# A two-layer block (causal attention, then a product-key mixture of 1024 experts): scale moved into the selecting matrix, the best sixteen of both tiles taken together, the maximum's steps spread over three bank pairs

## What is computed

```python
def reference(x, w_attn, w_proj, gamma, wq, keys, table_down, table_up):
    x = x + attention(layernorm(x), w_attn, w_proj)   # 16 heads of 8, one shared key and value head, causal
    x = x + ffn(layernorm(x), ...)
    return x

def ffn(x, gamma, wq, keys, table_down, table_up):
    xn = rmsnorm(x, gamma)
    q = (xn @ wq.T)                       # two halves, 8 heads, width 64
    sim = einsum('pbnhd,hkpd->pbnhk', q, keys)        # 2 x 32 similarities a head
    sx, ix = top_k(sim[0], 16);  sy, iy = top_k(sim[1], 16)
    all_scores = sx[..., :, None] + sy[..., None, :]  # 16 x 16 pairs
    scores, pk = top_k(all_scores, 16)
    indices = (ix * 32 + iy)[pk]
    h = einsum('bnd,bnhkd->bnhk', xn, table_down[indices])
    h = gelu(h) * softmax(scores)
    return einsum('bnhk,bnhkd->bnd', h, table_up[indices])
```

## Time and profile before

| | |
|---|---|
| median of 3 runs | 893.08 us |
| the profiled execution: its own time | 894.57 us |
| its span, first to last instruction | 892.8 us |
| mean granted TensorE clock | 0.935 of full |
| busy: TensorE | 716.4 us (80%) |
| busy: VectorE | 761.1 us (85%) |
| busy: ScalarE | 708.2 us (79%) |
| busy: GpSimd | 648.8 us (73%) |

### The profile page before, as it was taken

The page is one execution under the profiler, slowest core; times in us unless marked ns, Lnnn a source line. Parts: engine busy times, 40 slices in busy tenths (PEclk is TensorE's granted clock), DMA queues, the critical chain, the costliest instruction groups (busy, mean ns, idle before and its releaser), DMA issues.

```text
span 892.8 us, 20720 instructions
## 1 busy us (share of the span) xinstructions
PE 716.4 (80%) x5972; PEld 471.3 (53%) x6004; DVE 761.1 (85%) x2966; ACT 708.2 (79%) x961; POOL 648.8 (73%) x371
## 2 busy tenths in 40 slices
PE   3787787888979797888979797978889797967454
PEld 2653345564746465565646464655647463635333
DVE  4328699989999898999899898989899898969596
ACT  1364888989889898989989898989898888856371
POOL 2111586997979696988979696969979795969470
PEclk9797889999999999999999999999999998978676
DMA  6323021211203021212103020212112020100000
GB/s 169 52 39 71 1 54 26 58 25 26 56 10 72 0 64 18 57 25 44 38 10 72 0 67 15 57 25 57 25 27 55 10 68 1 31 1 19 0 1 12
DMA packets 34736, 32.52 MB, mean 36 GB/s; under 512 B 5521, under 2 KB 32785, under 8 KB 32977
## 3 DMA queue, kind: packets, MB, share of 16 engines
q1 hardware_dynamic: 34608, 32.12, 16.2%
q10 hardware_dynamic: 96, 0.02, 0.0%
HBM read 19.93 MB, written 5.24 MB: 28 GB/s over the span
## 4 chain that ended last, share of the span: by engine, by line
issue 32%; DVE 23%; PE 21%; POOL 11%; ACT 9%; DMA 1%; POOLq 1%; DVEq 1%; ACTq 0%; SPq 0%
POOL acc L503 9%; DVE prob L1027 8%; PE score L1325 4%; DVE late_scores L882 3%; ACT prob L721 3%; PE score L1340 3%; ACT late_scores L599 3%; DVE halves L876 2%; PE misc L1348 2%; PE misc L1249 2%; POOL pieces L490 1%; PE misc L1299 1%; DVE acc L1039 1%; PE score L1229 1%; PE score L1288 1%
## 5 line engine op out<-in xcount | busy, mean ns | idle before, releaser
L503 POOL TENSOR_TENSOR acc<-acc,prob 128x1024 f32<-128x1024 f32 x186 | 441.8, 2375 | 16.6 <-DVE prob L1027 0.5
L1027 DVE SCALAR_TENSOR_TENSOR prob<-score,cut,prob 128x1024 f32<-128x1024 f32 x256 | 317.9, 1279 | 23.4 <-ACT prob L721 22.0
L721 ACT ACTIVATE prob<-score,neg_lse,unit 128x1024 f32<-128x1024 f32 x256 | 302.0, 1204 | 23.4 <-PE score L1325 21.9
L1325 PE MATMUL score<-sel,pieces_t 128*128 128x512 f16 x512 | 165.2, 408 | 67.2 <-DVE prob L1027 64.2
L503 POOL TENSOR_TENSOR acc<-prob 128x1024 f32<-128x1024 f32 x31 | 73.2, 2362 | 105.9 <-DVE prob L1027 105.9
L626 ACT ACTIVATE probs<-score 128x512 f32<-128x512 f32 x192 | 109.9, 598 | 24.1 <-PE score L1231 20.2
L1325 PEld LDWEIGHTS score<-sel,pieces_t 128*128 128x128 f16 x512 | 39.9, 102 | 133.2 <-DVE prob L1027 121.3
L1288 PE MATMUL score<-xn_kept,wdt 128*128 128x128 f32 x480 | 85.0, 278 | 3.9 <-DVE prob L1027 3.5
L1288 PEld LDWEIGHTS score<-xn_kept,wdt 128*128 128x128 f32 x480 | 72.4, 191 | 29.7 <-issue 6.7
L1348 PEld LDWEIGHTS misc<-wu,gated_t 128*128 128x128 f32 x512 | 69.1, 200 | 13.8 <-DVE qk_rest L869 5.8
L1199 PE MATMUL score<-k_ahead,q_ahead 128*128 128x256 bf16 (+1 forms) x512 | 69.8, 249 | 6.8 <-DMA q_ahead<-q_scratch 4.3
(11 more groups left out here) (130 smaller groups left out, 1422.1 us busy)
## 6 DMA issues: line engine op xcount, KB each, us to landing
q_scratch<-qk_piece SPq DMA_DIRECT2D x16, 192.0 KB, 2.1
q_ahead<-q_scratch SPq DMA_DIRECT2D x16, 192.0 KB
q_stack<-q_scratch SPq DMA_DIRECT2D x16, 192.0 KB
xin<-x SPq DMA_DIRECT2D x16, 128.0 KB, 2.3
q_ahead<-q_scratch SPq DMA_DIRECT2D x16, 128.0 KB
q_stack<-q_scratch SPq DMA_DIRECT2D x16, 128.0 KB
xres<-x SPq DMA_DIRECT2D x16, 128.0 KB, 2.6
x_kept<-x SPq DMA_DIRECT2D x16, 128.0 KB, 2.0
```

What stands on the lines that cost most here:

```text
L503: eng.tensor_tensor(acc[:, j, :], so_far, prob[:, j * FH + h, :], ALU.add).then_inc(acc_added, 1)
L721: eng.activation(prob[:, g, :], score[g % BUFS][:, :], ACT.Exp, bias=neg_lse[:, j, h:h + 1], scale=unit[:, :]).then_inc(prob_made, 1)
L1027: eng.scalar_tensor_tensor(prob[:, g, :], score[g % BUFS][:, :], cut[:, j, h:h + 1], prob[:, g, :], ALU.is_ge, ALU.mult).then_inc(prob_mas ...
L1325: ins = eng.matmul(score[g % BUFS][:, cols], pieces_t[:, j, h, :], sel[:, cols], start=True, stop=True)
```

## The change

- `unit` becomes a power of two: the exponent bits of its inverse are kept and those of its own value, by integer masks in the prologue. The selecting matrix is scaled by it (`sel_unit`, bf16) and is used by `pair_scores` in place of the fp16 `sel`, so the heads' exponentials need no scale pointer. The cut, computed in the old units, is multiplied by `unit` (`scale_cut`, a new VectorE operation on 128x16).
- `shift_best`, `best_exp`, `sum_best`, `log_sum` and `log_sum_exp` handle both tiles at once. The shift stands behind gate 0 on VectorE and copies to `score[0]` instead of `misc[1]`; pair search of tile 0 is followed by tile 1's at once. `sum_best` stands ahead of gate 1, `log_sum_exp` between folds 0 and 1. On ScalarE `best_exp` stands after x2, the logarithm after all six steps of the maximum and ahead of both copies of pieces.
- The maximum's steps use `score[2]`, `[1]`, `[2]`, `[1]`, `[2]`, `[0]`. Step 0 is issued ahead of the value product, so it waits for all twelve attention exponentials, and its copy ahead of the logarithm for y. Step 5 waits for the shift. The projection comes after step 3, then step 4, acc of tile 1, step 5, pieces 0 and pieces 1.
- `copy_v` moves behind the second head's exponential. Head 0's scores wait for all six steps' copies.

```diff
+MAX_BANK = (2, 1, 2, 1, 2, 0)
...
-                eng.activation(prob[:, g, :], score[g % BUFS][:, :], ACT.Exp, bias=neg_lse[:, j, h:h + 1],
-                               scale=unit[:, :]).then_inc(prob_made, 1)
+                eng.activation(prob[:, g, :], score[g % BUFS][:, :], ACT.Exp,
+                               bias=neg_lse[:, j, h:h + 1]).then_inc(prob_made, 1)
...
 (ScalarE, iteration)
+                if m:
+                    max_scores_back(i + 2, 0)
                 if a:
                     invert_sums(i + 1)
                 if m:
-                    copy_v(i + 2)
-                    max_scores_back(i + 2, 0)
                     max_scores_back(i + 2, 1)
-                if f:
-                    best_exp(i, 0)
-                if m:
                     max_scores_back(i + 2, 2)
                     max_scores_back(i + 2, 3)
                 if a:
                     x2_back(i + 1)
                 if f:
+                    best_exp(i)
+                if m:
+                    max_scores_back(i + 2, 4)
+                    max_scores_back(i + 2, 5)
+                if f:
+                    log_sum(i)
                     pieces_back(i, 0)
-                if m:
-                    max_scores_back(i + 2, 4)
-                if f:
-                    log_sum(i, 0)
-                if m:
-                    max_scores_back(i + 2, 5)
-                if f:
                     pieces_back(i, 1)
...
                     pair_probs(i, 0, 0)
-                    best_exp(i, 1)
                 if p:
                     xhat_back(i + 3)
                 if f:
                     pair_probs(i, 0, 1)
-                    log_sum(i, 1)
+                if m:
+                    copy_v(i + 2)
+                if f:
                     pair_probs(i, 0, 2)
...
 (VectorE)
+            def shift_best(b):
+
+                firsts = score[0][:, 0:TILES * FH].rearrange("p (j h k) -> p j h k", j=TILES, k=1)
+                eng.wait_ge(pair_step, every(pair_step, b))
+                if later(b):
+                    eng.wait_ge(gated, at(gated, b - 1, 1))
+                eng.tensor_copy(firsts, best[:, :, :, 0:1]).then_inc(first_placed, 1)
+                eng.wait_ge(first_placed, every(first_placed, b))
+                eng.tensor_tensor(shifted[:, :, :, :], best[:, :, :, :],
+                                  firsts.broadcast_to([P, TILES, FH, TOPK]), ALU.subtract).then_inc(shifted_made, 1)
...
+            def scale_cut(b):
+
+                value = held(eng, every(cut_made, b))
+                eng.wait_ge(setup_dve, 1)
+                eng.wait_ge(cut_made, value)
+                eng.tensor_scalar(cut[:, :, :], cut[:, :, :], unit[:, :], None, ALU.mult).then_inc(cut_scaled, 1)
...
 (VectorE, prologue)
+                eng.tensor_scalar(unit_inv[:, :].bitcast(INT32), unit_inv[:, :].bitcast(INT32), EXPONENT, None,
+                                  ALU.bitwise_and).then_inc(unit_step, 1)
...
+                eng.tensor_scalar(unit[:, :], unit[:, :], 1.0 + 2.0 ** -12, None, ALU.mult).then_inc(unit_step, 1)
...
+                eng.tensor_scalar(unit[:, :].bitcast(INT32), unit[:, :].bitcast(INT32), EXPONENT, None,
+                                  ALU.bitwise_and).then_inc(unit_step, 1)
...
+                eng.tensor_scalar(sel_unit[:, :], sel[:, :], unit[:, :], None, ALU.mult).then_inc(sel_made, 1)
...
 (VectorE, iteration)
                     select_pairs(i, 0)
-                    shift_best(i, 0)
                     sum_pairs(i, 1)
                     select_pairs(i, 1)
                 if a:
                     make_y(i + 1)
                 if d:
                     gate(i - 1, 0)
+                if f:
+                    shift_best(i)
                 if a:
                     norm_x2(i + 1)
                 if p:
                     ln1(i + 3)
                 if f:
-                    sum_best(i, 0)
+                    bound_sizes(i)
+                    sum_best(i)
                 if d:
                     gate(i - 1, 1)
-                if f:
-                    shift_best(i, 1)
-                    log_sum_exp(i, 0)
-                if m:
-                    fold_max(i + 2, 0, 3)
-                if f:
-                    bound_sizes(i)
-                if m:
-                    fold_max(i + 2, 3, 4)
-                if f:
-                    sum_best(i, 1)
-                if m:
-                    fold_max(i + 2, 4, 5)
+                if m:
+                    fold_max(i + 2, 0, 1)
+                if f:
+                    log_sum_exp(i)
+                if m:
+                    fold_max(i + 2, 1, 2)
                 if f:
                     place_cut(i)
                 if m:
-                    fold_max(i + 2, 5, 6)
+                    fold_max(i + 2, 2, 4)
+                if f:
+                    scale_cut(i)
+                if m:
+                    fold_max(i + 2, 4, 6)
                 if f:
                     mask(i, 0, 0)
-                    log_sum_exp(i, 1)
                     mask(i, 0, 1)
...
 (TensorE, iteration)
+                if m:
+                    scores_for_max(i + 2, 0)
                 if a:
                     weigh_values(i + 1, 0, max_t_made, i + 1)
                     weigh_values(i + 1, 1, max_t_made, i + 1)
                 if m:
-                    scores_for_max(i + 2, 0, d)
-                    scores_for_max(i + 2, 1)
+                    scores_for_max(i + 2, 1, d)
+                    scores_for_max(i + 2, 2)
                 if d:
                     acc_transposes(i - 1, 0)
                 if m:
-                    scores_for_max(i + 2, 2)
                     scores_for_max(i + 2, 3)
                 if a:
-                    if f:
-                        eng.wait_ge(pair_step, at(pair_step, i, PAIR_STEPS + SUM_STEPS))
                     project_y(i + 1, y_t_made, i + 1)
+                if m:
+                    scores_for_max(i + 2, 4)
+                if d:
+                    acc_transposes(i - 1, 1, m)
+                if m:
+                    scores_for_max(i + 2, 5)
                 if f:
                     if a:
                         piece_transposes(i, 0, y_t_made, every(y_t_made, i + 1))
                     else:
                         piece_transposes(i, 0, sim_kept, every(sim_kept, i))
-                if m:
-                    scores_for_max(i + 2, 4)
-                    scores_for_max(i + 2, 5)
-                if f:
                     piece_transposes(i, 1, piece_t_made, at(piece_t_made, i, 1))
-                if d:
-                    acc_transposes(i - 1, 1, m)
```

More of the change, by code:

```diff
@@ L7 @@
 FP16 = mybir.dt.float16
+INT32 = mybir.dt.int32
 ALU = mybir.AluOpType
@@ L25 @@
 SIM_PEAK = float(2 ** 15)
+EXPONENT = 0x7f800000
 K_PIECE = (0, 0, 0, 1, 1, 2)
@@ L741, in prologue @@
                 xhat_back(2)
+                max_scores_back(1, 0)
                 invert_sums(0)
-                for w in range(2):
-                    max_scores_back(1, w)
+                max_scores_back(1, 1)
                 x2_back(0)
@@ L1307, in pair_scores @@
                     eng.wait_ge(piece_t_made, at(piece_t_made, b, j + 1))
+                    if not later(b):
+                        eng.wait_ge(sel_made, 1)
                 if g < 2 and not a:
@@ L1310, in pair_scores @@
                 elif g < 2:
+                    if m and g == 0:
+                        eng.wait_ge(max_kept, every(max_kept, b + 2))
+                    elif g == 0:
+                        eng.wait_ge(shifted_made, every(shifted_made, b))
                     if later(b):
@@ L1384, in prologue @@
                 xhat_transpose(2, qk_rest_made, 1)
+                scores_for_max(1, 0)
                 weigh_values(0, 0, max_t_made, 0)
                 weigh_values(0, 1, max_t_made, 0)
-                for w in range(2):
+                scores_for_max(1, 1)
+                project_y(0, xhat_t_made, 2)
+                for w in range(2, 5):
                     scores_for_max(1, w)
-                project_y(0, xhat_t_made, 2)
                 eng.wait_ge(setup_done, 2)
-                for w in range(2, WIDE_STEPS):
-                    scores_for_max(1, w)
+                scores_for_max(1, 5)
                 eng.wait_ge(y_t_made, every(y_t_made, 0))
```

92 lines of the change are left out of this document (47 added, 45 removed).

## The result

The changed kernel is slower. Its median is 911.20 us (4 runs, 908.01 to 911.98) against 894.27 us of the kernel before on the same chip (4 runs); the ratio is 1.0181, with a 95% interval of 1.0146 to 1.0216. I had forecast 889.8 us, a range of 879 to 899 and 0.17 for slower. The prediction is wrong.

A forecast was written before the change was run, and what follows sets the result against it. It took VectorE's work plus some 3 us of waits, set by a chain from x2 through xhat, as the bound. Turns -1.2, iterations 13 to 15 -1.3, -0.8, -1.0, prologue +1.0: -3.3, so 893.08 becomes 889.8 us; range 879 to 899.

The forecast's parts named there:

- What bounds the kernel now: One loop turn: VectorE works 46.04 of 49.60 us, TensorE at full clock; mask waits follow a chain from x2.
- part 5: ScalarE, log-sum and piece copies behind the joint sum: log 444.8, pieces 1 to 447.8, exponential 0 at 448.65.
- Part 1: VectorE, best sixteen handled together: net -0.4 us, y can start at 439.07, scaling of the cut some 0.12.
- Part 2: First maximum step ahead of the value product: wait 0.57, step 0.87, x2 late by 0.3 us.
- Parts 3 and 4: VectorE, shift behind first gate, second gate at 444.7, first fold 445.95, mask 0 at 450.6, 1.3 us ahead.
- Part 6: GpSimd, folds 0 and 1 beside xhat: xhat ends at 449.7 (449.15 to 450.15), 0.85 us later than now.
- Part 7: ScalarE, exponential 1 to mask 5 (9.10 us): shortened by 0.91, including four exponentials at 0.09 each.
- Part 8: TensorE, head scores: fp16 pieces times a bf16 matrix cost zero, at most +0.44 us a head.
- The sum: Per turn +0.85 (xhat) - 0.91 = -0.1 us; twelve turns -1.2; with later iterations and prologue, -3.3.
- The first rival: Loop turns: xhat not stretched further or hidden behind exponential 0, gain 0.6 to 0.8 a turn, 882.6 us; chance 0.28.
- The second rival: GpSimd, xhat between folds 0 and 2: folds block it fully, +0.7 us a turn, 899.4 us; chance 0.14.
- The third: ScalarE's exponentials: dropping the scale pointer saves nothing, turn grows by 0.26 us, 894.1 us; chance 0.1.

The follow-up runs named there:

- the filler: The changed kernel plus 14 unread 256-column TensorE products between the transposes of pieces 0 and pieces 1: 891.26 us, ratio 0.9968.
- the run that takes the scale out: The filler kernel with the exponentials' scale pointer and the fp16 selecting matrix restored and the cut unscaled: 904.50 us, ratio 1.0126.
- xhat and the order behind it: The filler kernel with first layer norm ahead of gate 0, and xhat made, transposed and copied ahead of xn: 877.29 us, ratio 0.9808.
- the kernel with the scale alone: The kernel before with only power-of-two unit, scaled bf16 selecting matrix, no scale pointer and the cut scaled: 895.32 us, ratio 1.0020.
- xhat first: The changed kernel with the first layer norm ahead of gate 0 on VectorE and xhat ahead of xn on GpSimd: 908.51 us, ratio 1.0177.

## Why the prediction was wrong

The step that failed is the one in "What bounds the kernel now" that took TensorE "at full clock" from the earlier trace rows and left it so. One turn of full clock was no sign of room: four of the twelve turns of that same profile lose clock for a moment, and the stretch of the earlier trace rows begins at 402.29, just where one such moment ends (398.87 to 402.27 at half clock). I took it as the pattern of all. I worked out when TensorE would do each piece of work, even that pieces 1 would be transposed behind a copy that ended at 445.95, and didn't ask what it would do in between. Every number of part 5 contained the gap: the second transposes could not begin before pieces 0 were copied, some 2 us after the first. The price, 1.2 to 2.4 us a turn (49.53 with the clock held up, 50.7 to 51.9 without), is in none of my terms or rivals, and my slower rival named another mechanism (GpSimd). The range ended at 899.

Point by point:

- **Part 1.** y at 439.07: it came at 450.98 - 12.02 = 438.96. Right. The scaling of the cut takes 0.22 us, not 0.12.
- **Part 2.** x2 0.3 us late: its statistics start at 454.14 - 12.02 = 442.12 instead of 441.88. Right. (The wait of 0.57 is 0.48 by its own two numbers, 430.91 - 430.43.)
- **Parts 3 and 4.** Second gate at 444.7, first fold at 445.95, mask 0 at 450.6: they came at 444.74, 445.87 and 450.95. Right but for mask 0, where the placing of the cut took 0.60 us instead of 0.18 beside GpSimd's operations (the earlier trace rows show the like for the combination): 0.94 ahead instead of 1.3.
- **Part 5.** Logarithm at 444.8, pieces copied by 447.8: 444.86 and 447.82. Exponential 0 came at 448.95 instead of 448.65. It waits for xn, whose transposes ran at half clock; with the filler it came 0.26 earlier.
- **Part 6.** xhat at 449.7, between 449.15 and 450.15: it ended at 449.96. Right, a little to the late side, and through the mechanism of the first iteration. The strict rule that I had quoted from the Trainium skill, page "SBUF — State Buffer" (section "SBUF: two separate sides"), would have it at 450.15 or after; the trace lies just under that, and shows each of the three operations stretched, as the rule says in kind.
- **Part 7.** 0.09 us an exponential: 91 ns. Four on the path up to mask 5 is right (0.39 by the run that takes the scale out); the 0.27 behind mask 5 was missing. With the clock up, exponential 1 to mask 5 takes 8.10 us, where the 0.91 of this part gives 8.19. The Trainium skill's page "ScalarE: Activation LUTs" (section "What ACT_TABLE_LOAD costs") has 93 ns for a pointer operand, and the trace agrees.
- **Part 8.** Mixed product at no cost: right (379 ns both).
- **The sum.** -0.1 us a turn: with the clock held up it is 49.53 against 49.57 in the typical turn. The errors inside it cancelled, which is luck: exponential 1 comes 26.98 after the key search instead of 25.80, 1.18 later where I had 0.85 (0.25 of that difference because xhat is later than taken), against 0.09 more between exponential 1 and mask 5 and 0.28 behind mask 5. I also rounded +0.85 - 0.91 = -0.06 to -0.1 before multiplying by twelve, so -1.2 should have been -0.7 and the forecast 890.3. Iteration 13 gave 0 instead of -1.3, iteration 14 -2.5 instead of -0.8, the end -2.0 instead of -1.0, what comes ahead of the turns +2.3 instead of +1.0: -2.2 together where I had -2.1. That agreement is luck too: each term was off by 1.0 to 1.7.

With the filler the whole is 891.3 us where 889.8 had been forecast, and the ratio is 0.9968 where 889.8 / 893.08 is 0.9963. The steps of the schedule came out nearly as worked out, though the agreement of their sum is partly luck. The clock was left out, and it was the larger effect by far.

The first rival (the gain comes through if xhat is early) also has its answer: xhat alone doesn't do it, because xn then takes its place; xhat and the order behind it do, 877 us. The second rival (the folds block GpSimd fully) was to be decided by xhat ending later than 449.8, and it ended at 449.96; but its price of +0.7 a turn isn't there with the clock held up, so the mark I had set for it was no sign of its cost. The third (the pointer saves nothing) and the fourth (the mixed product is slow) fall by the runs above.

## What to carry to other kernels

When a change moves waits between engines, write down what TensorE does in every stretch of the new order, its idle ones as well. This kernel had room for neither a 2 us gap followed closely by another, nor for a longer wait of TensorE for mask 0: each put the products behind it at half clock, on the path, in all or in some turns. A reordering that ties transposes to copies on another engine makes such gaps; check the granted clock of every turn before any other reading, in the kernel before as well. And when two producers compete for the same stretch (xhat and xn beside the folds), moving one moves the delay to the other; what helps is that neither is needed at once. A few moved calls on each engine did that on the old kernel and gave 1.4%.

## What the runs showed of the hardware that I had not expected

- The clock's fall depends on more than the gap right before it. TensorE idle for 2.10 us and again for 0.77 lost full clock in all twelve turns; with the first filled (14 products) it lost it in one turn of twelve, with the second filled (6 products) in five, with 6 in the first in eleven. In the changed kernel the fall came in the second stretch or right behind it, while the work in between still ran at full clock. After the fall TensorE stayed at half clock through nearly unbroken work (5.98 us busy of the 6.51 from 459.99 to 466.50 above).
- The same turn, with the same order and the same waits ahead of the fall, can keep the clock or lose it. In the filler kernel iterations 9 and 10 both have 0.57, 0.77 and 1.20 us of idle time in a row, and only iteration 10 loses it. In the kernel with the scale alone every third turn lost it, in the changed kernel all do, and the lengths go 50.7, 50.96, 51.9 and repeat; so a turn picked for reading should have its neighbours beside it.
- xn's two operations beside folds 0 and 1 took 3.35 us instead of 1.58, the folds themselves stayed at 1.21 and 1.22. Beside the folds it was mostly GpSimd that waited. But VectorE waited too, above all in its small operations: the cut's placing took 0.60 us instead of 0.18 in the changed kernel, the combination 0.58 instead of 0.22 and fold 1 1.52 instead of 1.23 in the kernel before, and the last operation of `ln1` 1.07 instead of 0.19 once it stood beside GpSimd's low pieces (xhat first).
